# Shifted rows of the last up-sampling: fetched as 112 and 15 rows of a tile instead of 127, a whole neighbouring tile as one transfer instead of two

## The reference

```
for lvl in range(4):                                   # every 2**lvl-th token
    outs.append(_mha(query[:, ::2**lvl, :], in_proj_w[lvl], ..., out_b[lvl]))
current = outs[-1]
for lvl in range(2, -1, -1):
    current = _upsample_linear(current, outs[lvl].shape[1])    # twice as many tokens
    current = current @ up_w[lvl].T + up_b[lvl] + outs[lvl]
x = _layernorm(x + current)
h = silu(x @ w1.T * s1) * (x @ w2.T * s2)
h = gelu(gelu(h @ h1.T * t1) @ h2.T * t2)
out = _layernorm(x + h @ w3.T * s3)
```

## Time and profile before

| | |
|---|---|
| time, median of 3 runs | 3690.92 us (3688.53 to 3693.14) |
| profiled execution, its own time | 3691.8 us |
| its span, mean granted clock | 3690.0 us, 0.963 |
| PE busy | 3413.8 us, 93% |
| DVE busy | 2531.4 us, 69% |
| ACT busy | 2533.0 us, 69% |
| POOL busy | 1042.7 us, 28% |
| DMA | 269.88 MB, mean 73 GB/s |

### The profile page before, as it was taken

How to read it: one execution, slowest core, us unless ns; L and a number is a source line. 1 busy time by engine, 2 the same in 40 slices (tenths; PEclk the granted TensorE clock), 3 DMA queues, 4 the chain that set the end, 5 groups by cost and what they waited for, 6 DMA issues and landing times. The chain is left out here.

```text
span 3690.0 us, 58638 instructions
## 1 busy us (share of the span) xinstructions
PE 3413.8 (93%) x20635; PEld 1407.3 (38%) x20635; DVE 2531.4 (69%) x4805; ACT 2533.0 (69%) x3266; POOL 1042.7 (28%) x1060
## 2 busy tenths in 40 slices
PE   5899899999899999989989988679999999999998
PEld 3333333333333333333333322234444445444444
DVE  4798888988988988988898889523334333333333
ACT  2699789789889889889889868634444444444443
POOL 2243444454353354364363342300000000000000
PEclk6899999999999999999999999889999999999999
DMA  4533333333333333333342332200000000000000
GB/s 150 164 102 96 108 100 100 104 103 97 104 113 90 105 120 86 109 118 85 106 127 79 100 106 85 65 16 13 13 13 24 13 12 12 13 14 23 12 13 13
DMA packets 240831, 269.88 MB, mean 73 GB/s; under 512 B 59012, under 2 KB 206596, under 8 KB 239904
## 3 DMA queue, kind: packets, MB, share of 16 engines
q1 hardware_dynamic: 231280, 257.11, 23.7%
q10 hardware_dynamic: 9216, 8.39, 0.7%
HBM read 159.75 MB, written 101.45 MB: 71 GB/s over the span
## 5 line engine op out<-in xcount | busy, mean ns | idle before, releaser
L958 ACT ACTIVATE a_probs<-a_p_s,a_unit_now 128x1024 f32<-128x1024 f32 x1360 | 1439.7, 1111 | 216.0 <-PE a_p_s L1283 212.0
L1064 DVE TENSOR_REDUCE a_part_max<-a_p_r 128x1 f32<-128x512 f32 x2048 | 1290.3, 678 | 155.2 <-PE a_p_r L1296 149.0
L1296 PE MATMUL a_p_r<-a_k_st,a_q_st 48*128 48x512 f16 (+2 forms) x2944 | 878.1, 381 | 119.7 <-DVE a_part_max L1064 49.7
L1655 PE MATMUL p_h<-f_h_hi,f_w_hi 128*128 128x512 f16 x2048 | 776.3, 379 | 4.4 <-issue 4.4
L1655 PE MATMUL p_h<-f_h_lo,f_w_hi 128*128 128x512 f16 x2048 | 776.2, 379 | 0.0
L1313 PE MATMUL a_p_o<-a_probs,a_v_aug 128*17 128x512 f32 (+2 forms) x5888 | 738.1, 583 | 1.3 <-ACT a_probs L958 0.4
L1283 PE MATMUL a_p_s<-a_q_st,a_k_st 50*128 50x512 f16 (+2 forms) x2944 | 660.1, 376 | 46.1 <-DMA a_q_st<-a_neg_bf 28.0
L1296 PEld LDWEIGHTS a_p_r<-a_k_st,a_q_st 48*128 48x128 f16 x2944 | 219.0, 94 | 1016.6 <-DVE a_part_max L1064 665.6
L1517 ACT ACTIVATE f_h_f<-p_h,f_sc_now 128x512 f32<-128x512 f32 x256 | 175.9, 687 | 518.3 <-PE p_h L1655 518.3
L1064 DVE TENSOR_REDUCE a_row_max<-a_p_r 128x1 f32<-128x512 f32 (+2 forms) x672 | 418.6, 677 | 69.9 <-PE a_p_r L1296 68.8
L1464 POOL TENSOR_TENSOR f_rstd<-f_var_eps,f_minus_half 128x1 f32<-128x1 f32 x64 | 35.0, 547 | 1242.0 <-DVE f_var_eps L1610 1242.0
(11 more groups left out here) (157 smaller groups left out, 4434.4 us busy)
## 6 DMA issues: line engine op xcount, KB each, us to landing
qk_scratch<-a_qk_room SPq DMA_DIRECT2D x288, 128.0 KB
a_q_st<-qk_scratch SPq DMA_DIRECT2D x240, 96.0 KB, 2.5
a_w_lo<-wqkv_inner SPq DMA_DIRECT2D x30, 768.0 KB, 5.9
a_a_lo<-a_attn SPq DMA_DIRECT2D x448, 32.0 KB, 2.0
a_k_st<-qk_scratch SPq DMA_DIRECT2D x64, 192.0 KB, 3.8
a_o_lo<-wo_inner SPq DMA_DIRECT2D x24, 512.0 KB, 3.5
a_qk_room<-wf SPq DMA_DIRECT2D x23, 512.0 KB, 3.9
a_k_st<-qk_scratch SPq DMA_DIRECT2D x112, 96.0 KB, 2.4
```

Source lines behind the costliest of these rows:

```text
L958: act.activation(probs[:, s % 2, 2 * p:2 * p + 2, :], p_s[:, 2 * p:2 * p + 2, :], ACT.Exp, scale=unit_now[:, lvl:lvl + 1]).then_inc(exp_do ...
L1064: dve.reduce_max(out, src, AX.X).then_inc(max_read.sem, 1)
L1296: ins = pe.matmul(p_a[:, r * size:(r + 1) * size], q_st[rows_of(j, ROWS), query_at:query_at + 128], k_st[rows_of(j, ROWS), key_at:key_at + ...
L1655: ins = pe.matmul(out, a, c, start=first and n == 0, stop=last and n == len(terms) - 1)
```

## The change

`neighbours` cuts the runs differently. Tiles 1 and 6 come as one transfer of 128 rows instead of 64 + 64. In tiles 0 and 7, each run is cut into a part whose count is a multiple of 16 and the rest: 1 + 112 + 15 rows, and 112 + 15 + 1. Tiles 2 to 5 stay at 64 + 64. Fetch 0 covers tiles 0 and 1, fetch 3 tiles 6 and 7, so these two have other transfers, and still four each; fetches 1 and 2 are as they were. The same bytes go to the same places. No other engine's work or order is touched, and the line numbers behind the function rise by 4.

```
     if len(parts) == 1:
-        parts = [(0, parts[0][1], 64), (64, parts[0][1] + 64, 64)]
-    assert len(parts) == 2
-    return parts
+        return parts if n in (1, 6) else [(0, parts[0][1], 64), (64, parts[0][1] + 64, 64)]
+    split = []
+    for to, src, size in parts:
+        whole = size // 16 * 16
+        split += [(to, src, whole)] * (whole > 0) + [(to + whole, src + whole, size - whole)] * (size > whole)
+    assert len(split) == 3
+    return split
```

## The result

The changed kernel takes 3623.97 us (median of 4 runs, 3622.58 to 3629.09), the kernel before beside it 3691.13 us (3688.53 to 3693.14): a ratio of 0.9821 with a 95% interval of 0.9804 to 0.9838, 67 us less. The forecast was 3641 us in a range from 3627 to 3665: right in direction and in the cause, and 17 us too small in size.

A forecast was written before the change was run, and what follows sets the result against it. TensorE, VectorE and ScalarE take turns as the limit in attention, with stalls behind 127-row transfers on one DMA engine. 15.2 + 25.2 + 10.5 + 2.9 - 4.2 = 49.6 us, giving 3641 us; range 3627 to 3665 (8 in 10).

The forecast's parts named there:

- (3): Rival: 112 and 15 rows run on one engine like 127, both stalls stay, nothing changes: 3691 us; chance 0.06.
- (4): Rival: odd pieces do not spread and each holds SyncE's queue 2.2 us; slower by 8 to 13 us, 3701 us; chance 0.03.
- Stall A: After fetch 0: late neg transfer holds ScalarE's L950, TensorE waits for L950; removal worth 15.2 us, 7 times 2.2.
- Half-clock time: Stretch at clock 0.50 behind stall A; running it at full clock was to win 0.3 us in each of 7.
- what comes back: Ordinary waits on VectorE and ScalarE behind the removed ones: 0.3 us for each of 14 stalls, 4.2 us lost again.
- Stall B: After fetch 3: TensorE's score matmuls wait for the neg transfer behind the 127-row backlog; removal worth 25.2 us, 7 times 3.6.
- the end: End of attention, last batch: GpSimd's last sum is held by the store of x behind fetch 3; 2.9 us to win.
- clock term: Half-clock stretch behind stall B, 1.2 us each from ScalarE's pace; with 0.3 behind stall A, 10.5 us over seven batches.
- Rival (1): A removed stall is replaced by other waits; half of each stays and the clock still falls: 23 us, 3668 us; chance 0.15.
- The clock (2): Rival: only the stalls go, the clock falls at another small gap: 39 us, 3652 us; chance 0.75 together with the main case.

The follow-up runs named there:

- the row of sizes: Changed kernel with the 127 rows cut otherwise: 113 + 14 3680.8 us, 97 + 30 3666.4, 61 + 66 3631.12, 126 + 1 3622.85, beside 112 + 15 3623.03.
- the kernel with 113 + 14: Changed kernel with the 127-row run cut at 113 + 14 instead of 112 + 15: 3680.8 us, ratio 0.9985 to the kernel before.
- the new fetch 0: Alone: kernel before with only fetch 0 (tiles 0 and 1) cut the new way, fetch 3 as before: 3658.47 us against 3685.26, ratio 0.993.
- the third room: Kernel before with three rooms for the negated maxima (neg_bf) instead of two: 3677.91 us against 3689.17. The same on the changed kernel: 3625.12 us.
- the filler: Kernel before with 14 more 512-column matmuls with ones on TensorE at each of seven stalls B, their product overwritten: 3667.33 us, ratio 0.9954.
- halves: Two kernels, each with one fetch cut the new way: fetch 0 alone 3658.47 us (26.8 less), fetch 3 alone 3649.73 us (35.5 less).
- the new fetch 3: Alone: kernel before with only fetch 3 (tiles 6 and 7) cut the new way, fetch 0 as before: 3649.73 us, ratio 0.9901.
- the one in the changed kernel: Changed kernel with five more 512-column matmuls with ones ahead of L1215 of the second fine unit: 3619.43 us beside 3623.03.

## Where the prediction was right, and which step was too small

**The cause.** Right. That 127 rows run on one engine, that 112 and 15 spread, and that the issues behind them are as a rule not held is shown by the DMA share after fetch 3 (0.07 before, full and then done after), by the issue times (1.59 and 1.69 us, but for two fetches 0; 2.1 and 2.2 forecast), and by the row of sizes. Rivals (3) and (4), by which the odd pieces do not spread, are out; the kernel with 113 + 14 is what (3) describes, and it stays within 1 to 10 us of the kernel before.

**Stall A.** This is the step that failed: "Value: the 15.2 us of the earlier trace rows, 7 times 2.2." Its chain was right link by link (5.03 us forward for 5.0; the `neg` transfer in time, with the wait gone), but its value was read from TensorE, which only waits for ScalarE there. ScalarE stood in the same place 20.9 us, as its row in the forecast's own timeline said (2.88 us against TensorE's 2.07), and 4.9 us more on `wf`, the next transfer of the late queue. The sum of ScalarE's two waits, 20.9 + 4.9 - 0.2 = 25.6 us, would have been the better value; measured alone, A is worth 26.8 us (20 to 32). Half-clock time was to add 7 x 0.3 = 2.1 us to the 15.2; after what comes back the forecast had 15.2 us for A. These 11.6 us are most of what is missing. For 6.5 of them, 21.7 less 15.2, two kernels show that they are ScalarE's: the new fetch 0 moves L950 forward by 21.7 us, and the third room does the same 21.7 us by another way, and loses 14.1 of them again where the next late transfer stands. The other 5 are a sum of three things that no run takes apart: the wait for `wf`, the half-clock stretch behind A, and new falls of the clock (below).

**Stall B and the end.** 25.2 + 8.4 (clock) + 2.9 - 2.1 (half of what comes back) = 34.4 us forecast, 35.5 measured. The wait itself went as said. Its clock term was too small, at 1.2 us a stretch from ScalarE's pace alone, where the filler finds 2.4 (1.6 to 3.3). But the two terms are not to be added. 25.2 + 16.8 + 2.9 = 44.9 us would be the whole, where 35.5 was measured (28 to 46), and the matched starts say the same more sharply: without the stall L950 moves forward by 28.7 us across B (27.8 to 30.2 in eight executions), which holds the wait and the stretch together. The filler alone gives 12.1 of them with the stall in place, so the 25.2 us of waiting are worth some 17 once the clock stays up (an estimate, from one execution with the filler). That the sum came out within 1 us is therefore in part luck: the wait was taken too large and the clock too small.

**What comes back.** At TensorE nothing of the 4.2 us shows: its waits behind the two places are the ordinary ones of 0.2 us, and the `neg` transfer has 1.8 us from the end of its issue to the first matmul that needs it, without a wait. At ScalarE something does: the waits for `xt_inner` and `a_attn` behind B, 5.8 us and 7.5 us more than before. What they cost was not measured; they are one reason why a wait of 25.2 us can be worth less. Rival (1), a stall that is replaced at the same engine, is out for this change. It is what happened with the third room. (Its counter-argument, DMA engines 0.34 busy, was read from the stretch at A; at B they are full until 450 us.)

**The clock (2).** Partly seen. The clock does fall at smaller gaps that were covered before (468 us in the first batch); counted in stretches of 1 us up to 2420 us, 274 us are below 0.9 before and 176 us after. It cost less than the two large terms that went. One such fall has a price that the traces show. In the 18 us behind A, the step of the lead takes one of two values in each batch: in the second batch it is 1.43 us in the execution whose clock stays at 1.00 there, and -0.03 to 0.15 in the seven whose clock falls to 0.50 there for 3 to 4 us. Over the seven batches of the eight executions with the new fetch 0, the clock falls in 31 of 56 places, and a fall takes 1.2 to 1.5 us. Whether it comes at a given place differs from one execution of a kernel to the next. How much of A's 27 us is the clock behind A itself was not measured: no filler was tried there.

**The sum against the measurement.** 15.2 + 34.4 = 49.6 us forecast. 26.8 + 35.5 = 62.3 us in halves, 61.3 together on one chip, 67.2 in the first comparison. So 11.6 us are A and 1.1 us B. The last 5 us go with the kernel before, which took 3691 us beside the first result and 3684 to 3685 beside these, while the changed kernel repeated to 1 us; why is open.

## What to carry to other kernels

When a stall is to be taken away, look at the waits of every nearly full engine that stands in it and at the next waits behind it on the same queue, not only at those of the engine at whose rows one came upon it. At stall A the larger one, ScalarE's, gave the better size. The half-clock stretch behind a stall has a price too, but the two overlap: at stall B, 25.2 us of waiting and 12.1 of clock made 28.7 together. Choose the row counts of transfers so that they divide well over 16 engines (here 112, 126 and 128, and not 127, 113 or 97): in these runs a large prime piece blocked one engine and the small urgent transfer behind it. And a wait removed on its own at the receiver met the next late transfer of that queue.

## What was not expected of the hardware

- The issue behind a transfer on one engine is held. In fetch 3 that is 1.8 to 2.4 us behind 127 rows, 1.9 to 4.1 behind 113, 1.1 to 1.6 behind 97, and 0.4 to 0.8 behind 61, where 0.44 is the time behind 112. In fetch 0 113 rows hold less than 127. Why the order of the two differs between the fetches is open, and so is why an issue of fetch 0 is held in the fourth and the last batch of the changed kernel.
- The direct steps of one cause repeat closely, summed over seven batches: 21.7 us across A in each of the eight executions with the new fetch 0, and 27.8 to 30.2 us across B in the eight with the new fetch 3. The rest varies by up to 10 us between them. It varies between two executions of the same kernel too: the changed kernel profiled again had a span of 3630.9 us instead of 3620.8, and its direct steps were the same 21.7 and 29.0 us. The clock fell in one and not in the other at the same place, which is 664 us, just behind the place of stall A in the second batch. First the one of 3620.8 us, then the one of 3630.9:

```profile
664.00:668.00 4.00, 4.00 (x44) 2.50 (x41) 4.00 (x10) 4.00 (x5) 0.00 (x0) 1.00 0.33 50
```

```profile
664.00:668.00 4.00, 4.00 (x33) 2.30 (x26) 3.71 (x9) 3.62 (x5) 0.00 (x0) 0.57 0.08 9
```

- A full clock need not be time won. The filler in the kernel before won 16.8 us, the one in the changed kernel raised the clock from 0.50 to 1.00 over the stretch at 468 us and won nothing that can be measured; why was not tested.
